# A fused attention and local-attention stack: new issue order, semaphores per projection bank, another spread of K's norm and another mask tiling

## Time and profile before

| | us |
|---|---|
| median of 3 runs | 1754.83 |
| lowest, highest | 1753.96, 1762.12 |
| span of the profiled execution | 1764.5 |
| TensorE busy in it | 1603.1 (91%) |
| VectorE busy | 1226.0 (69%) |
| ScalarE busy | 1147.8 (65%) |
| GpSimd busy | 1002.6 (57%) |

### The profile page before, as it was taken

How to read it: one execution, slowest core, us unless ns; L and a number is a source line. 1 busy time by engine, 2 the same in 40 slices (tenths; PEclk the granted TensorE clock), 3 DMA queues, 4 the chain that set the end, 5 groups by cost and what they waited for, 6 DMA issues and landing times. The chain is left out here.

```text
span 1764.5 us, 75677 instructions
## 1 busy us (share of the span) xinstructions
PE 1603.1 (91%) x33590; PEld 1308.3 (74%) x33590; DVE 1226.0 (69%) x1912; ACT 1147.8 (65%) x2115; POOL 1002.6 (57%) x757
## 2 busy tenths in 40 slices
PE   5969899988999999999998999998999999999987
PEld 4557778777777777777787787787777777778765
DVE  7766677675767767767776776776777677677662
ACT  2246677765676776766776677676676676767644
POOL 2155566664656666655675665685566585566551
PEclk9989999998999999999999999999999999999987
DMA  3266665675566567566657656657665665665650
GB/s 129 57 168 136 156 151 131 155 182 132 126 150 155 123 154 204 139 143 154 141 135 184 167 129 152 150 128 184 164 148 133 161 143 137 157 155 123 150 123 25
DMA packets 98567, 252.96 MB, mean 143 GB/s; under 512 B 30016, under 2 KB 36288, under 8 KB 97472
## 3 DMA queue, kind: packets, MB, share of 16 engines
q1 hardware_dynamic: 98240, 248.12, 59.1%
HBM read 44.59 MB, written 2.10 MB: 26 GB/s over the span
## 5 line engine op out<-in xcount | busy, mean ns | idle before, releaser
L803 DVE SCALAR_TENSOR_TENSOR UV<-ps,veca,rope 128x512 f32<-128x512 f32 x768 | 530.7, 744 | 187.5 <-PE ps L381 163.7
L1210 POOL TENSOR_TENSOR KK<-UV 128x512 f32<-128x512 f32 x192 | 241.6, 1280 | 396.3 <-DVE UV L803 393.0
L955 ACT ACTIVATE sq<-ps 128x512 f32<-128x512 f32 (+1 forms) x400 | 228.1, 583 | 269.5 <-PE ps L381 176.8
L1210 POOL TENSOR_TENSOR Qtb<-UV 128x512 f32<-128x512 f32 x192 | 243.1, 1288 | 92.4 <-DVE UV L803 92.4
L381 PE MATMUL ps<-xh,wh 128*128 128x256 f32 x768 | 244.4, 318 | 4.4 <-DVE UV L803 2.5
L381 PEld LDWEIGHTS ps<-PT,V 64*64 64x64 f32 x12288 | 199.1, 137 | 45.0 <-issue 38.6
L1229 POOL TENSOR_TENSOR E<-E,ri 128x1024 f32<-128x1024 f32 x96 | 182.7, 1903 | 78.6 <-DVE ri L876 73.2
L381 PE MATMUL ps<-PT,V 64*64 64x32 f32 x12288 | 215.7, 222 | 8.0 <-issue 5.0
L381 PE MATMUL ps<-xh,wl 128*128 128x256 f32 x768 | 217.1, 283 | 0.9 <-issue 0.9
L381 PE MATMUL ps<-xl,wh 128*128 128x256 f32 x768 | 217.2, 283 | 0.0
L1220 POOL TENSOR_TENSOR E<-E,mx 128x1024 f32<-128x1024 f32 x96 | 182.7, 1903 | 58.6 <-DVE mx L870 58.6
(11 more groups left out here) (128 smaller groups left out, 3113.9 us busy)
## 6 DMA issues: line engine op xcount, KB each, us to landing
V<-Vs SPq DMA_DIRECT2D x672, 128.0 KB
KK<-KK SPq DMA_DIRECT2D x384, 128.0 KB
Qtb<-Qtb SPq DMA_DIRECT2D x384, 128.0 KB, 2.4
rope<-in_c_rope SPq DMA_DIRECT2D x48, 512.0 KB
raw<-in_Wqkv SPq DMA_DIRECT2D x6, 1536.0 KB, 7.8
V<-Vs SPq DMA_DIRECT2D x96, 64.0 KB
V<-V SPq DMA_DIRECT2D x96, 64.0 KB, 2.0
wo<-in_Wo SPq DMA_DIRECT2D x6, 512.0 KB
```

What stands on the lines that cost most here:

```text
L803: e.scalar_tensor_tensor(UV[:, p % 2, slot, :].rearrange("p (i t) -> p i t", i=2), ps[:, half, :].rearrange("p (i t) -> p i t", i=2), veca ...
L955: return e.activation(out, in_, f, **kw)
L1210: e.tensor_tensor(dst, u, v, op).then_inc(s["rot_done"], 1)
```

## The change

1. **Order.** `SCHEDULE` is a new list. A token may now end in `-1` (a group behind) or `+2`; iterations run from -2 to N+2. The stages are cut elsewhere: the second half of b (`b_pt2`, `b_pt3`, `b_att2`, `b_att3`, `b_oto1`, `b_xb`) and the later c parts (`c_h1`, `c_h2`, `c_gelu1`, `c_gelu2`, `c_down`, `c_fin`) run one iteration later than before.
2. **Semaphores.** `proj_done`, `sq_done`, `mul_done` become one each for bank 0 (`projx_done`, `sqx_done`, `mulx_done`) and bank 1 (`projy_done`, ...). `SQUARE_FIRST` says which passes are squared before they are multiplied: pass 3 in bank 0, passes 1 and 3 in bank 1; the others are multiplied first.
3. **Norm of k.** `ind` fills eight rows of each quarter instead of four, so the sum stands twice. `Rhl = R * is_low - Rh`, one DVE instruction, holds `-Rh` in one half of the rows and `R - Rh` in the other; `sel` has signs -1 and +1, and 4 products of 128 rows do the spread, 2 per bank. POOL's `Rl` is gone.
4. **Mask.** Always 8 products of 64x32 per chunk; `fourb` is gone.
5. `b_att0` takes the wait for `e_done` that `b_pt0` had; the tail's transposes are split over three iterations.

```diff
+SCHEDULE = """a_v0 b_pt2-1 a_vs0 a_rot3-1 b_pto2-1 c_h1-1 a_v1 c_gelu1-1 b_xb-1 c_hm1-1 b_pt3-1 a_vs1 c_h2-1 b_pto3-1 b_rcq
+    c_gelu2-1 w_l1-1 a_x0 b_lnq a_y0 b_att2-1 a_xh+1 a_mx0 b_att3-1 a_my0 b_rqt w_l2-1 a_sqx0 c_hm2-1 b_oto1-1 a_x1
+    w_h0 a_sqy0 a_rot0 w_l0 c_wh-1 b_s0 b_s1 b_rq a_y1 a_xl+1 c_wo a_mx1 b_scale0 b_s2 a_sqy1 b_max0 b_s3 a_sqx1
+    b_sub0 c_xb c_xs a_norm0 a_my1 a_rot1 b_scale1 b_exp0 c_down-1 a_rck b_sum0 b_nrm0 b_max1 c_mu a_x2 a_lnk c_wl-1
+    c_zsq c_var a_halo a_rh a_mx2 a_y2 c_rs c_zn b_pt0 a_sqx2 b_pt1 a_rl b_pto0 b_pto1 b_sub1 a_sp0 a_my2 a_kn0 c_zh
+    a_sqy2 c_zl b_att0 b_exp1 c_fin-1 b_att1 a_sp1 b_oto0 a_kn1 a_x3 c_h0 b_sum1 a_sqx3 a_rot2 a_xs+2 a_y3 b_nrm1
+    b_wo a_mx3 a_sqy3 a_my3 c_gelu0 c_hm0 w_h1 w_h2 a_norm1""".split()
+SQUARE_FIRST = ((3,), (1, 3))
...
-            def a_sp(m, i):
-
-                if i:
-                    e.wait_ge(s["rkb_done"], m * 2 + 1)
-                else:
-                    e.wait_ge(s["rl_done"], m + 1)
-                for x in range(2):
-                    for b in range(2):
...
-                        ins = mm(ps[:, b, i * T:(i + 1) * T], sel[rows, q, :], (Rh, Rl)[x][rows, :], x == 0, x == 1,
-                                 tile_position=(q * W, 0))
+            def a_sp(m, b):
+
+                bank = "xy"[b]
+                if b == 0:
+                    e.wait_ge(s["rhl_done"], m + 1)
+                e.wait_ge(s["sq%s_done" % bank], m * 4 + (3 if m else 2))
+                e.wait_ge(s["mul%s_done" % bank], m * 8 + (6 if m else 4))
+                for i in range(2):
+                    ins = mm(ps[:, b, i * T:(i + 1) * T], sel[:, 2 * b + i, :], Rhl[:, :])
...
-                        if chosen:
-                            rows = slice(r * DH, r * DH + W)
-                            mm(ps[:, 2 + r, :].rearrange("p (j k) -> p j k", j=HP), fourb[rows, :],
...
+                        rows = slice(r * DH, (r + 1) * DH)
                         for w in range(NW):
...
+                            v = 2 * r if first and w == 0 else 1
+                            mm(ps[w * W:(w + 1) * W, 2 + r, :].rearrange("p (j k) -> p j k", j=HP), identb[rows, r * DH:r * DH + W],
+                               mask[rows, v:v + 1, :].broadcast_to([DH, HP, KEYS]), True, False, skip_group_check=True,
+                               tile_position=(r * DH, w * W))
...
+            def a_rl(m, _):
+
+                e.wait_ge(s["rh_done"], m + 1)
+                if m:
+                    e.wait_ge(s["rkb_done"], m * 2)
+                e.scalar_tensor_tensor(Rhl[:, :], R[:, 0, :], is_low, Rh[:, :], ALU.mult,
+                                       ALU.subtract).then_inc(s["rhl_done"], 1)
+
             def a_kn(m, b):
 
-                e.wait_ge(s["rkb_done"], m * 2 + 2)
+                e.wait_ge(s["rkb_done"], m * 2 + b + 1)
```

More of the change, by code:

```diff
@@ L70, in part @@
 def part(token):
-    name, plus = (token[:-2], 1) if token.endswith("+1") else (token, 0)
-    return name.rstrip("0123456789"), int(name[-1]) if name[-1].isdigit() else 0, LAG[token[0]] - plus
+    name, ahead = (token[:-2], int(token[-2:])) if token[-2] in "+-" else (token, 0)
+    return name.rstrip("0123456789"), int(name[-1]) if name[-1].isdigit() else 0, LAG[token[0]] - ahead
 def run(parts, tail):
-    for it in range(-1, N + 2):
+    for it in range(-2, N + 3):
         for name, i, lag in map(part, SCHEDULE):
@@ L82, in run @@
         if it >= N:
-            for g in range(G - 2) if it == N else (G - 2, G - 1):
+            for g in (range(G - 3), (G - 3,), (G - 2, G - 1))[it - N]:
                 tail(g)
@@ L111, in constants @@
     first = seen & ~((np.arange(P)[:, None] < W) & (kk[None, :] < W))
-    mask = np.where(np.stack([first, seen, np.roll(first, W, 0)], 1), 0.0, NEG)
-    ind = np.zeros((P, W), f32)
+    mask = np.where(np.stack([first, seen, np.roll(first, DH, 0)], 1), 0.0, NEG)
+    ind = np.zeros((P, W + 1), f32)
     sel = np.zeros((P, HQ, P), f32)
     for hq in range(HQ):
-        ind[hq * W:(hq + 1) * W, hq] = 1
-        for q in range(HQ):
-            sel[W * q + hq, q, hq * W:(hq + 1) * W] = 1
+        for row, sign in ((hq, -1), (W // 2 + hq, 1)):
+            ind[hq * W:(hq + 1) * W, row] = 1
+            for q in range(HQ):
+                sel[W * q + row, q, hq * W:(hq + 1) * W] = sign
+    ind[:, W] = a >= W // 2
     blk = (np.arange(P)[:, None] // DK == np.arange(P)[None, :] // DK).astype(f32)
@@ L515, in b_s @@
                     e.wait_ge(s["x1_done"], G1)
-                chosen = 0 if n % G == 0 and c == 0 else 1
+                first = n % G == 0 and c == 0
                 if i % 2 == 0:
@@ L740, in _ @@
             e.tensor_copy(identb[:, :], ident[:, :]).then_inc(s["sel_done"], 1)
-            for r in range(2):
-                rows = slice(r * DH, r * DH + W)
-                e.tensor_copy(fourb[rows, :].rearrange("p (g k) -> p g k", g=NW),
-                              ident[rows, rows].unsqueeze(1).broadcast_to([W, NW, W])).then_inc(s["sel_done"], 1)
             e.tensor_scalar(cen[:, :], ident[:, :], -1.0 / D, None, ALU.add).then_inc(s["sel_done"], 1)
@@ L827, in clamp @@
                 e.wait_ge(s["norm_done"], step * 2 + side + 1)
-                if step and side == 0:
-                    e.wait_ge(s["rl_done"], step)
-                elif step:
+                if step and side:
                     e.wait_ge(s["rqt_done"], step)
@@ L940, in _ @@
             m_add(2)
+            a_rl(0, 0)
             a_kn(0, 0)
@@ L946, in _ @@
             m_add(3)
[L948 removed]
+            run({"a_mx": a_mx, "a_my": a_my, "a_rck": a_rck, "a_rl": a_rl, "b_rcq": b_rcq, "a_kn": a_kn, "b_rq": b_rq, "b_scale": b_scale,
                  "b_max": b_max, "b_sum": b_sum, "b_xb": b_xb, "c_xb": c_xb, "c_zn": c_zn,
@@ L1205, in a_rot @@
                 q = 2 * (p % 2)
-                for half, (x, y, op, count) in enumerate(((0, 2, ALU.subtract, 3), (3, 1, ALU.add, 4))):
-                    e.wait_ge(s["mul_done"], m * 16 + 4 * p + count)
+                for half, (x, y, op) in enumerate(((0, 2, ALU.subtract), (3, 1, ALU.add))):
+                    e.wait_ge(s["mulx_done"], m * 8 + 2 * p + half + 1)
+                    e.wait_ge(s["muly_done"], m * 8 + 2 * p + half + 1)
                     dst = (Kt if p < 2 else Qt)[:, half, q:q + 2, :]
```

112 lines of the change are left out of this document (58 added, 54 removed).

## The result

The changed kernel takes 1811.78 us (median of 4 runs, 1801.47 to 1817.52) where the kernel before took 1757.11 on the same chip: a ratio of 1.031, 95% interval 1.027 to 1.035. Forecast were 1721, a range from 1678 to 1764 and a chance of 0.15 for slower. The profiled execution took 1801.47, with a span of 1799.5, 35.0 more than the 1764.5 of before.

What follows compares the result with a forecast made beforehand. TensorE was nearest to a bound, so the pitch per group decided: 32.5 us quiet plus 0.8 of disturbances, 33.3 against 34.0 over 46 groups, giving 1731 profiled, 1721 by the median; range 1678 to 1764.

Steps and rivals of the forecast that it cites:

- new pitch: Time per group over 46 groups: 33.3 us forecast against 34.0 on average before.
- The walk: New list laid in order on the engines, each part starting when free and its waits met: 32.5 us quiet.
- three stretches: `a_v0` until DVE hears of `b_s1`, 12.85 us; DVE until `a_kn1` ends, 15.9; then until `a_v0` again, 3.7.
- quiet pitch: Time of a group without disturbances: 32.5 us forecast against 32.8 before.
- `a_rl` on DVE: Norm of k in DVE's stretch: 0.45 us plus 0.8 waiting for POOL's `b_sub1`, 1.25 in all.
- The separate semaphores cost nothing: Semaphores per bank priced at nothing; what they permit is in the in-order layout of the list.
- should mostly go: PE's waits for q's copies, 0.5 us a group and in 26 groups before, mostly disappear.
- The load of W2: On SP, third group of a layer: waits for a later `c_down`, some 9 us; costs 0.3 us, five times.
- The sum: 12.85 + 15.9 + 3.7 + 0.05 = 32.5 us, plus 0.8 disturbances: 33.3 a group, 32 to 34 us less overall.
- disturbances: Per group above the quiet time: 1.2 us before (q waits 0.5, issue stalls 0.6, layer boundaries), 0.8 forecast.
- The slower case: Rival, q loop: late `a_rot3` makes q 1.6 us late each time; pitch 34.9, 41 us more, 1796; chance 0.14.
- The engines don't meet: Rival: `a_rl` doesn't wait for POOL; pitch 0.8 us lower, 37 us less, 1684; chance 0.22.
- become the bound: Rival: ACT's and DVE's chains overlap better, leaving PE's work as limit, 31 us a group; 1617; chance 0.04.

Runs made afterwards that it cites:

- e18: Changed kernel without TensorE's implied (redundant) waits and with the wait for `b_scale1` (`e_done`) back in `b_pt0`: 1.003 of the kernel before.
- e16: Kernel before with one TensorE wait moved, that for `b_scale1` (`e_done`), from `b_pt0` to ahead of `b_att0`: 1.026 of the kernel before.
- e15: Changed kernel with TensorE's implied waits taken out (`a_v`, `a_x1`, `a_x2`, `a_y1`, `a_y2`, `a_sp`): 1.017 of the kernel before.
- e13: Kernel before with ten redundant TensorE waits per group added, no new semaphore or order: 1.001 of the kernel before.
- e9: Kernel before with only the semaphores per bank and the wait for `e_done` in its new place, old order: 1.042 of the kernel before.

## Why the prediction was wrong

**What bounds the kernel.** Right as far as it went. "So the question is the new pitch" was the step too far: I read the issue stalls of the earlier trace rows as "stalls that nothing in the trace explains" and then carried them over as a constant. (The wait for zs, which I put at 0.79 us once a group, is 26.7 / 36 = 0.74 in 36 of 48 groups; nothing hangs on it.) They were 2% of the time in the kernel before, the longest total in the waits, and had a place (23 of 23 over 0.5 us) that could have been found from the same trace.

**The walk.** Right to 0.4 us in all three stretches (12.5, 15.8 and 3.9 against 12.85, 15.9 and 3.7), and so in the quiet pitch, 32.2 against 32.5. Part of that is luck: the 12.5 hold a stall of 0.54 us that the walk didn't have, and PE stood still for 0.24 us at `b_pt0` instead of 1.2. The quickest group of e18 takes 31.4 us, so the walk of the list itself was about a microsecond too long.

**The parts with a price.** `a_rl` on DVE takes 1.43 us in the median (forecast 1.25) and 0.48 at its shortest (0.45, although the row of `c_fin` in the earlier trace rows has 485 ns): the two engines do meet, as the earlier trace rows said. The median is 0.95 above the shortest, where I had taken 0.8; the mechanism was right. In 44 of the 48 groups POOL was inside an operation when `a_rl` started, and `a_rl` ended 0.27 to 0.29 us behind the end of that operation, whatever was left of it (0.63 to 1.53 us); in the other four POOL was free and it took 0.48. In the rows above `Rhl`, from 1000.22 to 1001.42, ends 0.3 us behind POOL's split of w1, from 999.46 to 1001.13. The rule of the Trainium skill (SBUF — State Buffer, Who interferes with whom) agrees. The mask takes 0.23 us from its start to the first score product (987.36 to 987.59), near the lower bound of 0.2. "The separate semaphores cost nothing" is wrong for the edit as it was made: I didn't cost the wait for `b_scale1`, which moves with it. By the values that it waits for, it costs nothing at either place, and the rows of e16 confirm that; the cost goes with when the next block of instructions moves.

**Queues.** q's copies were waited for in 16 groups instead of 26 (18.9 us against 23.9): the direction holds, but not "should mostly go". The load of W2 does wait for `c_down` on SP:

```profile
SPq L284 <- PE ps L385: 56.3, 5, 13.8
```

Five times, as I had it, and with 11 us each rather than 9; no wait of PE for q is longer than 2.7 us.

**The sum.** This is the term that failed: "Of the 1.2 of disturbances the q waits of 0.5 should mostly go, and I leave 0.8." They are 2.7 a group, not 0.8: 46 x 1.9 = 87 us. With 0.8 the measured quiet pitch of 32.2 would have given 33.0 and a gain of some 46 us. Of the 2.7, stalls of instruction supply are 2.1, where the 0.8 held about 0.6 for them, and the longer time at half clock adds up to 0.5.

**The rivals.** The slower case had the right sign and about the right time (1796) and the wrong mechanism: q was not late. No rival named TensorE's own supply of instructions. "The engines don't meet" is refuted by the 44 of 48. PE didn't become the bound through its work, but through its standing still.

**What stays open.** The traces show that the packet moves later when the wait stands in front of `b_att0`. They don't show why. The Trainium skill (Runtime: NRT & Kernel Launch, Instruction fetch mechanics) has the sequencer start a fetch itself, so one that is held in front of `b_att0` would start it later; that fits the packet's 2.4 us and was only argued. There the moved wait is a second one beside that for `pts_done`, ahead of the same product, and becomes a record of its own (one more a group in e16), which it isn't in `b_pt0`; a redundant second wait at that place alone, with the first left in `b_pt0`, would tell the place from the pairing, and wasn't run. Nor was it shown why the redundant waits cost 1.4% in the new order (e15) and none in the old (e13). In the new order `a_sp0` with its waits stands right ahead of `b_att0`, in the old one it comes behind `b_att1`; and e15, with the moved wait in front of `b_att0` but `a_sp0`'s redundant ones gone, has 5.9 us of stalls at the attention products, where e16 has 19.4. So in the new order the moved wait alone doesn't bring those stalls, and what e18 gains over e15 lies elsewhere, the largest part in the score products (33.0 us against 41.9). The changed kernel with its redundant waits and only the moved one put back wasn't run. e18 still has 69.7 us of stalls, and is no faster than the kernel before: the forecast gain wasn't reached by any kernel that computes the same values.

## What to carry to other kernels

When a kernel issues thousands of products of 30 to 60 columns, count instructions per microsecond as you count bytes: TensorE's program is a stream with a supply of its own, and a row "issue" in its waits is a cost that a new order can multiply. In the kernels here it paid to keep a second wait of TensorE, even one long met, out of the place right ahead of a dense run, and to put it behind the first instruction of the part before; whether that holds in other kernels has to be tried. When waits are rewritten in a change, compare them one by one: the move of one cost 2.6% here in the old order, more than the new order brought in any kernel with the full set of products.

## What the runs showed of the hardware

- TensorE's instructions come in packets of 16 KB, one for 256 records. The long stalls named issue sit at one position modulo 256 (67 of 69 in the changed kernel) and end 1.2 to 1.9 us after a packet's landing.
- A wait that is met without any delay can still cost 2.6% (e16, interval 1.8 to 3.4%), and the next packet moves later with it, while ten others a group cost 0.1% (e13, interval -0.2% to +0.5%).
- After a stall of 1.56 us with PE busy on either side, the granted clock was 0.54 and then 0.50 in the following 7 us. Between 150 and 1680 us the kernel before had 11 stalls named issue of over 1 us and 2 of them followed by such a stretch, e16 22 and 18, e9 29 and 20; why so few in the kernel before is open.
- A VectorE operation with both inputs in SBUF took 0.48 us for 128x256 elements when GpSimd was free at its start (4 groups), and otherwise ended 0.27 to 0.29 us behind the GpSimd operation that was running (44 groups, 0.91 to 1.82 us).
